# Two edits to a two-layer AdaLN program: the experts' back half moved into the next chunk's front, and a reciprocal root as one power on POOL

## What is computed

```python
h = _layernorm(x) * (1 + ca) + sa
x = x + ga * _L0_attn_ref(h, ...)
h = _layernorm(x) * (1 + cb) + sb
x = x + gb * _L0_ffn_ref(h, ...)

def _L0_attn_ref(x, ...):                 # 16 heads of 8
    x_norm = _layernorm(x, gamma, beta)
    q, k = x_norm @ w_q, x_norm @ w_k;  v = x @ w_v
    q = _l2_normalize(q);  k = _l2_normalize(k)          # per token and head: 64 norms a partition
    resonance = 0.5 + 0.5 * tanh((q k^T - 0.27) * 15)
    modulation = resonance * gate_q[..., :, None] * gate_k[..., None, :]
    return (modulation @ v) @ w_o + b_o

def _L0_ffn_ref(x, controller, f1, bias, f2):   # groups of 32 tokens, 32 experts x 4 sets = 128 slots
    logits = einsum('bgtd,des->bgtes', grouped, controller) + tie
    perm = (logits == max(logits, axis=-3))               # the token that each slot takes
    dispatched = einsum('bgtd,bgtes->bgesd', grouped, perm)
    inner = relu(einsum('bgesd,desf->bgesf', dispatched, f1) + bias)
    intermediate = einsum('bgesf,esfd->bgesd', inner, f2)
    return einsum('bgesd,bgtes->bgtd', intermediate, perm)
```

## Time and profile before

| | |
|---|---|
| median of 3 runs | 1460.92 us (1458.93 to 1463.24) |
| the profiled execution | 1462.04 us, its span 1460.0 us |
| mean granted clock | 0.916 |
| busy: PE, DVE, ACT, POOL | 85%, 75%, 65%, 36% of the span |
| first attention | about 24 to 446 us |
| experts | 446.6 to 724.3 us |
| second attention, second feed-forward part | behind it |

### The profile page before, as it was taken

One profiled execution on the slowest core, in us unless ns is written; L12 is line 12 of the kernel. 1 busy time (PEld: TensorE's weight loads), 2 busy tenths in 40 slices (PEclk: granted clock), 3 DMA queues, 4 the chain that ended last, 5 costly groups with the idle time before them and its releaser, 6 DMA issues. The chain is left out here.

```text
span 1460.0 us, 39907 instructions
## 1 busy us (share of the span) xinstructions
PE 1246.1 (85%) x13658; PEld 845.9 (58%) x13658; DVE 1090.6 (75%) x2971; ACT 949.6 (65%) x1308; POOL 526.1 (36%) x739
## 2 busy tenths in 40 slices
PE   2588888888885787787769999999937999999998
PEld 1345555555543667575635555555515877777776
DVE  2789999999965565655679999999746677777763
ACT  0388888888882534444428888888845666676675
POOL 1233333333321021211223333333304665565553
PEclk7699999999997797878769999999968999999999
DMA  3411111111001110100020000000000000000000
GB/s 81 149 35 34 32 32 32 32 32 32 25 9 47 29 36 11 45 3 16 2 91 17 12 14 14 14 11 14 12 3 1 8 15 7 14 14 14 7 15 23
DMA packets 44749, 37.82 MB, mean 26 GB/s; under 512 B 5008, under 2 KB 43472, under 8 KB 44144
## 3 DMA queue, kind: packets, MB, share of 16 engines
q1 hardware_dynamic: 44656, 36.56, 8.7%
HBM read 32.21 MB, written 4.34 MB: 25 GB/s over the span
## 5 line engine op out<-in xcount | busy, mean ns | idle before, releaser
L1960 ACT ACTIVATE a_probs<-psum_all 128x1024 f32<-128x1024 f32 x256 | 248.0, 1022 | 88.0 <-PE psum_all L1875 88.0
L474 ACT ACTIVATE probs<-psum_all,biases 128x1024 f32<-128x1024 f32 x256 | 270.9, 1113 | 45.8 <-PE psum_all L385 45.0
L2348 PE MATMUL psum_all<-ffn_hi,weights_r 128*128 128x512 f32 x704 | 286.5, 407 | 9.9 <-POOL ffn_lo L2308 5.7
L2348 PE MATMUL psum_all<-ffn_lo,weights_r 128*128 128x512 f32 x704 | 280.4, 398 | 0.0
L2308 POOL TENSOR_TENSOR ffn_lo<-ffn_full,ffn_hi 128x512 fp32r<-128x512 f32 x144 | 189.6, 1325 | 128.2 <-ACT ffn_hi L2433 87.6
L2348 PEld LDWEIGHTS psum_all<-ffn_hi,weights_r 128*128 128x128 f32 x704 | 133.6, 190 | 51.4 <-DVE ffn_full L2563 9.2
L2348 PEld LDWEIGHTS psum_all<-ffn_lo,weights_r 128*128 128x128 f32 x704 | 134.1, 190 | 28.6
L398 PE MATMUL psum_all<-probs,vpad 128*32 128x257 f32 x2048 | 140.4, 392 | 0.3 <-ACT probs L474 0.3
L1889 PE MATMUL psum_all<-a_probs,vpad 128*32 128x256 f32 x2048 | 137.0, 385 | 0.1
L2445 ACT ACTIVATE ffn_full<-psum_all,scales 128x512 f32<-128x512 f32 x128 | 88.2, 689 | 71.6 <-PE psum_all L2348 71.3
L2308 DVE TENSOR_TENSOR ffn_lo<-ffn_full,ffn_hi 128x512 fp32r<-128x512 f32 x64 | 55.0, 859 | 81.9 <-ACT ffn_hi L2448 81.9
(11 more groups left out here) (222 smaller groups left out, 2752.9 us busy)
## 6 DMA issues: line engine op xcount, KB each, us to landing
a_mod_gate<-modulation_table SPq DMA_DIRECT2D x64, 128.0 KB, 2.9
a_mod_norm<-modulation_table SPq DMA_DIRECT2D x32, 128.0 KB, 3.0
X<-in_x SPq DMA_DIRECT2D x32, 128.0 KB, 2.8
f<-in_f SPq DMA_DIRECT2D x2, 2048.0 KB, 10.1
e_mod_norm<-modulation_table SPq DMA_DIRECT2D x32, 128.0 KB, 2.9
out<-X SPq DMA_DIRECT2D x16, 256.0 KB, 2.3
e_gates<-modulation_table SPq DMA_DIRECT2D x32, 64.0 KB, 2.7
weights<-in_h SPq DMA_DIRECT2D x2, 1024.0 KB, 8.0
```

Source lines behind the costliest of these rows:

```text
L474: nc.scalar.activation(probs[:, c % 4, :, :, 0:T].rearrange("p r k q -> p (r k) q"), SC[c % 2].rearrange("p (a q) -> p a q", q=T), ACT.Tan ...
L1960: nc.scalar.activation(probs[:, c % 4, :, :, :].rearrange("p r k q -> p (r k q)"), SC[c % 2], ACT.Exp, scale=float(np.float32(1.0) / np.sq ...
L2348: ins = nc.tensor.matmul(dst, weights[:, w0:w0 + P], part[layer][:, k, :], start=first and i == 0, stop=last and i == len(parts) - 1)
```

## The change

In attention_0 the steps 2 to 9 of newton_step go. floor_norms keeps the first (with another scale), and a new POOL function root makes rnorm with one tensor_tensor of pow on 128x64. It stands in POOL's list between modulate(b+3) and gate_out(b). turned_out moves from the head of the next step to a place ahead of the splits. The two stacks become one tile whose parts are written by one cast, one subtraction and two copies. In experts_0 the chunks become one list of 42 steps without a loop: at step i the front works on batch i, and the back on chunk m with its work spread over 8 steps, s = (i - 9) mod 8. first_matrices lie in s 0 and 1, second_matrices in s 2 and 3, turn_back and hand_back in s 4 to 7. The turns of h and of the choice share a bank and one copy; scores and outputs share a bank; takenT, sent and given are kept twice, h and mod_norm four times instead of eight. The slots are numbered set first, so that results_out writes 8 neighbouring columns.

```diff
+            def root(n):
+                pool.wait_ge(norm2c_done, n + 1)
+                wait(pool, qkn_done, n)
+                wait(pool, gate_in_done, n)
+                nc.gpsimd.tensor_tensor(rnorm[:, :], norm2c[:, :], minus_half[:, :], ALU.pow).then_inc(rnorm_done, 1)
...
                     norm_1(b + 3)
                     modulate(b + 3, 1 - p)
+                if there(b + 2):
+                    root(b + 2)
                 if there(b):
                     gate_out(b, p)
...
+            def floor_norms(n):
+                dve.wait_ge(norm2_done, n + 1)
+                wait(dve, rnorm_done, n)
+                nc.vector.tensor_scalar(norm2c[:, :], norm2[:, :], NORM_FLOOR, SPLIT_SCALE ** -2, ALU.max, ALU.mult).then_inc(norm2c_done, 1)
 
             def scale(n):
-                dve.wait_ge(newton, n * RSQRT_STEPS + RSQRT_STEPS)
+                dve.wait_ge(rnorm_done, n + 1)
...
-                nc.vector.tensor_copy(qstack[p][:, :, 0:4:2, :], twice(0))
-                nc.vector.tensor_copy(kstack[p][:, :, 0:2, :], twice(1)).then_inc(hi_done, 1)
+                nc.vector.tensor_copy(part(p, 0), normed()).then_inc(hi_done, 1)
...
-                nc.vector.tensor_tensor(qstack[p][:, :, 1:4:2, :], twice(0), qstack[p][:, :, 0:4:2, :], ALU.subtract)
-                nc.vector.tensor_tensor(kstack[p][:, :, 2:4, :], twice(1), kstack[p][:, :, 0:2, :], ALU.subtract).then_inc(stacks_done, 1)
+                nc.vector.tensor_tensor(part(p, 1), normed(), part(p, 0), ALU.subtract).then_inc(lo_done, 1)
+
+            def double(n, p):
+                dve.wait_ge(lo_done, n + 1)
+                nc.vector.tensor_copy(stack[p][:, 1, :, 2:4, :], stack[p][:, 1, :, 0:2, :])
+                nc.vector.tensor_copy(stack[p][:, 0, :, 3:1:-1, :], stack[p][:, 0, :, 0:2, :]).then_inc(stacks_done, 1)
...
-                newton_of(1)
+                if next_:
+                    floor_norms(b + 2)
                 if new:
                     keys_out(b + 1, 1 - p)
-                newton_of(2)
...
                 if next_:
                     scale(b + 2)
                     gate_sums(b + 2)
+                if ahead:
+                    turned_out(b + 3, 1 - p)
+                if next_:
                     split_high(b + 2, p)
                     split_low(b + 2, p)
+                    double(b + 2, p)
```

TensorE's list of the experts after the change, and the new results_out and SP order:

```diff
+            for i in range(STEPS):
+                m, s = back(i)
+                before, at = back(i - 1)
+                if i <= B:
+                    turn(i)
+                if at in QUARTERS:
+                    hand_back(before, 2 * (at - 4) + 1, min(i, B))
+                if s in (0, 1):
+                    first_matrices(m, 2 * s)
+                    first_matrices(m, 2 * s + 1)
+                if s in (2, 3):
+                    second_matrices(m, 2 * (s - 2), min(i - 1, B))
+                if s in QUARTERS:
+                    turn_back(m, 4 * (s - 4))
+                    turn_back(m, 4 * (s - 4) + 1)
+                if front(i):
+                    score(i)
+                if front(i - 1):
+                    send(i)
+                if s in (2, 3):
+                    second_matrices(m, 2 * (s - 2) + 1, min(i, B))
+                if s in QUARTERS:
+                    turn_back(m, 4 * (s - 4) + 2)
+                    turn_back(m, 4 * (s - 4) + 3)
+                    hand_back(m, 2 * (s - 4), min(i + 1, B))
...
-                last = copy(given[:, :, slots].rearrange("p g e -> p e g"), given_banks(r)[s].rearrange("p (e g) -> p e g", g=CG))
+                last = copy(given[m % 2][:, :, slot:slot + EB], B_SLOTS[s].rearrange("p (e g) -> p g e", g=CG))
...
+            for n in range(HB):
+                load(n)
+            load_gates(0)
+            for n in range(HB, B):
+                if n % CB_ == 0 and n >= 3 * CB_:
+                    load_gates(n // CB_ - 2)
+                load(n)
```

More of the change, by code:

```diff
@@ L872, in _, with load, load_gates @@
-            for j in range(HB):
-                load(0, j)
-            chunk(0)
-            with sp.Fori(1, NCHUNK - 1) as c:
-                chunk(c)
-            chunk(NCHUNK - 1)
+            def load(n):
+                wait(sp, mod_loaded, 16 * n)
+                wait(sp, h_done, n - HB + 1)
+                sp.dma_start(mod_norm[n % HB][:, :, :], rows_of(n, ROW_CB0, 2)).then_inc(mod_loaded, 16)
+            def load_gates(m):
+                wait(sp, delta_done, m * CB_)
+                for j in range(CB_):
+                    sp.dma_start(gates[:, j, :], rows_of(m * CB_ + j, ROW_GB0, 1)).then_inc(gates_loaded, 16)
@@ L993, in _ @@
-            chunk(0)
-            with pe.Fori(1, NCHUNK - 1) as c:
-                chunk(c)
-            chunk(NCHUNK - 1)
-        def results_out(eng, copy, done, c, r, s0):
-            wait(eng, given_psum, c * ROUNDS + (r + 1))
+            for i in range(STEPS):
[13 more added lines that the diff above has]
+                    turn_back(m, 4 * (s - 4) + 1)
+                if front(i):
+                    score(i)
+                if front(i - 1):
+                    send(i)
[5 more added lines that the diff above has]
+                    hand_back(m, 2 * (s - 4), min(i + 1, B))
@@ L1055, in _, with front_out, sent_out @@
-            chunk(0)
-            with act.Fori(1, NCHUNK - 1) as c:
-                chunk(c)
-            chunk(NCHUNK - 1)
+            def front_out(i):
+                wait(act, turned, i + 1)
+                wait(act, logits_psum, i - 1)
+                wait(act, sent_psum, i - 2)
+                part = slice(0 if front(i) else T, 2 * T if front(i - 1) else T)
+                nc.scalar.copy(hT_taken[i % 2][:, part], bank[0][:, part]).then_inc(turned_done, 1)
+            def sent_out(n):
+                wait(act, sent_psum, n + 1)
+                wait(act, turned_back, (n // CB_ - 1) * TB_)
+                by_group = psum[:, 4 * 512:8 * 512].rearrange("p (g n) -> p n g", g=TG)
+                for t in range(TT):
+                    g0 = (n % CB_ * TT + t) * TG
+                    last = nc.scalar.copy(sent[n // CB_ % 2][:, :, g0:g0 + TG], by_group[:, t * SLOTS:(t + 1) * SLOTS, :])
+                last.then_inc(sent_done, 1)
@@ L1060, in _, with root @@
         @block.gpsimd
         def _(pool):
-            def root(c, j):
-                n = count(c, j)
+            def root(n):
                 wait(pool, moments_done, n + 1)
@@ new lines, in _ @@
+            wait(dve, w_loaded, 16 * len(dram["experts_loads"]))
+            centre(0)
+            for n in range(2):
+                modulate(n)
+                centre(n + 1)
+            for i in range(STEPS):
+                m, s = back(i)
+                before, at = back(i - 1)
+                if at in QUARTERS:
+                    gate(before, 2 * (at - 4) + 1)
+                if s in (0, 1):
+                    add_bias(m, 2 * s)
+                    add_bias(m, 2 * s + 1)
+                if s in (2, 3):
+                    results_out(dve, nc.vector.tensor_copy, given_dve, m, 2 * (s - 2), 0)
+                if s in QUARTERS:
+                    turned_out(dve, nc.vector.tensor_copy, givenT_dve, m, 4 * (s - 4))
+                if front(i + 2):
+                    modulate(i + 2)
+                if front(i):
+                    choose(i)
+                if s in QUARTERS:
+                    turned_out(dve, nc.vector.tensor_copy, givenT_dve, m, 4 * (s - 4) + 2)
+                    gate(m, 2 * (s - 4))
+                if front(i + 3):
+                    centre(i + 3)
+                if s in (2, 3):
+                    results_out(dve, nc.vector.tensor_copy, given_dve, m, 2 * (s - 2) + 1, 0)
```

486 lines of the change are left out of this document (197 added, 289 removed).

## The result

The kernel after takes 1758.07 us (median of 4 runs, 1754.84 to 1763.53), the one before 1459.93 us beside it (4 runs, 1458.87 to 1463.24): ratio 1.204, interval 1.200 to 1.208. The prediction was 1733 us, slower, with case A's own range of 1650 to 1830 and a range for 8 in 10 of 1440 to 1840.

A forecast was written before the change was run, and what follows sets the result against it. No engine was taken as full; a loop between TensorE and VectorE bounds the attention. Profiled 1462.0 us + 322 (attention) - 50 (experts) = 1734, so median 1733; 8 in 10 range 1440 to 1840.

The forecast's parts named there:

- case A: Attention, the forecast itself: the power costs by the column, 10.1 us for 64; 1733 us in all, chance 0.68.
- Part 1, the power: Attention, POOL: one 64-column power replaces eight VectorE steps and takes 10.1 us, from a line through widths 2 and 4.
- the addition's pace: POOL: columns beyond the first cost 2.1 ns each, as in a plain addition, so the 64-column power takes 0.83 us.
- B: Rival, attention: the power is cheaper by the column in a long run, about 5 us; step 16 us, 1537 in all; chance 0.12.
- C: Rival, attention: the power costs 0.83 us; step 11.0 us, 1374 us in all; chance 0.17.
- Part 2, the loop: Attention: work queued behind root on POOL waits, so the step becomes 22.2 us against 12.15; +322 us over 32 roots.
- Part 3, the splits: Attention, VectorE: one cast, one subtraction and two copies take 1.7 us instead of 2.0, covered by TensorE's projection.
- Part 4, the experts: Experts: the back of one chunk overlaps the front of the next; 227 us against 277.7, -50 us.
- 24 shared steps at 6.3 us: Experts: steps with front and back together, TensorE 5.9 us plus 0.4 for waits; 151 us in all.
- The first front, 40.2 us: Experts: the first chunk's front alone, from 446.6 to L925 at 486.78 us in the profile of before.
- The last back, 36 us: Experts: the last chunk's back alone, 38.7 us less 4 for the results and plus 1 for fewer banks.
- Rival D: Experts: the overlap does nothing or harms, the stage stays at 278 us; 1783 us with the 10.1 us power; no separate chance.

The follow-up runs named there:

- widths2: Kernel before with ten more POOL instructions in its setup, powers on 2 to 128 columns and multiplications on 2, 64 and 128: 1486.91 us.
- root_mult: Kernel after with root as a multiplication of the same operands instead of a power, not a usable result: 1403.14 us, ratio 0.959.
- root_32: Kernel after with the power on 32 of root's 64 columns and a multiplication on the rest, not a usable result: 1596.2 us.
- newton_after: Kernel after without the power, the nine newton steps back on VectorE, the last two between and behind the halves of xn: 1418.88 us, ratio 0.970.
- layout_only: Kernel before with only the slots numbered set first, so results_out writes runs of 8 columns, no overlap: 1446.82 us, ratio 0.992.

## Why the prediction was right, and where it was off

**Part 1, the power.** Right. 10.56 us against 10.1, between the ends. The choice of the line through the two widths over the addition's pace decided the case. The slope was 160 ns a column and not 153: from 2 to 4 columns is a short base to draw a line from. The rule of the Trainium skill (GPSIMD Engine Reference, section Performance versus the Vector engine: about 2.6 cycles an element for a tensor_tensor of two inputs) fits the multiplications of widths2 (2.1 ns a column) and not the powers (160 ns). Rivals B and C, which needed a power of 5 us and of 0.83 us, are out with the 10.56 us of L523. root_mult, C's case made by force, did give C's step, 10.95 against 11.0; its 1403 us against C's 1374 is the experts' missing gain. B's loop held too: with the 5.7 us of root_32 its sum gives 5.7 + 10.1 + 1 = 16.8, and that step is 16.98.

**Part 2, the loop.** Right in its order and nearly in its size. Counted from the start of a root, the forecast and two neighbouring steps (the second has its values at 342.63 and the next root at 345.41 in VectorE's and POOL's timelines):

| | forecast | step at 301.05 | step at 322.64 |
|---|---|---|---|
| power ends | 10.1 | 10.6 | 10.6 |
| xn ends | 12.9 | 13.3 | 13.3 |
| values start | 19.4 | 18.8 | 20.0 |
| next root | 22.2 | 21.6 | 22.8 |

Up to xn the chain ran 0.4 us late because of the power. For TensorE coming back cold I had taken "slow at first and fast at the end"; the real loop does the faster and the slower kind by turns, and their means are 19.4 for the values and 22.2 for the step, the forecast. That the means agree to a tenth is luck: neither kind is the step that I summed, and the 0.4 us that the chain is late at xn is made up behind it, where the sum had 6.5 us and the two steps take 5.5 and 6.7. With the clock up throughout the sum said 20.3; no step in the middle of the loop is that short. TensorE's idle before the turn was put at 9 us and is 9.7; VectorE's waits were put at some 8 us and are 322.3 / 31 = 10.4. The attention's sum is +309 against +322: the step of before had been counted as 12.15 from one pair of rows (which in fact start 12.19 apart), where its mean is 12.26, and the mean of after is 22.06 with the shorter steps at the loop's ends. That makes 0.25 x 32 = 8; most of the rest is one interval fewer (31, -9.8), less the 5 us that filling and draining add.

**Part 3, the splits.** 0.45 + 0.73 and two copies at about 0.20 each, 1.6 us against 1.7, and covered. What I said of hT and xnT, that moving them would fill idle time of the old loop, fits newton_after, which is 0.85 us a step shorter than the kernel before; the move is one of three things that differ there.

**Part 4, the experts.** Mis-sized: -15 in place of -50. The step that held is results_out: 0.69 us a copy forecast, 0.685 measured on VectorE, and layout_only shows that this term brings 13.9 of the 15 us. These failed:
- 24 shared steps at 6.3 us. They took 173.5 / 24 = 7.2. TensorE's busy time was put at 5.9 and is 152.87 / 24 = 6.4, since the clock came to 0.83 and not to the 0.88 which 5.9 supposes; the waits were put at 0.4, and TensorE's idle is 0.86. Together +22 us. All of it lies in the six steps with second matrices, with their waits for the four banks: from turn to turn they took 66.3 us, 11.0 each, and the other 18 took 6.0 each, less than forecast.
- The first front, 40.2 us, taken over unchanged from before. It took 43.5 (756.0 to 799.5): the turns of the choice and of h now go through one chain with the copy, and from the fourth batch on each takes 3.6 to 3.8 us from turn to turn, where the kernel before took 2.3 to 3.3. In each such step TensorE stands 0.68 us for the copy and 0.48 us for the choice. The shared bank and copy, which the forecast counted as a saving, thus seem to cost time here; that was read from the waits and not tried.
- The last back, 36 us. It took 46.5. I gave +1 us for the fewer banks; with one set of four, every round behind the first stands 1.6 to 1.7 us for the copies of the round before, and its matmuls run cold, 18.9 us for the four rounds against 7.5 in layout_only:

```profile
987.32 3.69 PE L936 MATMUL psum_all<-e_relued,f 32*128 32x64 f32 x64 [1.59 <-DVE e_slots L998]
...
992.71 3.69 PE L936 MATMUL psum_all<-e_relued,f 32*128 32x64 f32 x64 [1.70 <-DVE e_slots L998]
```

Rival D, that the experts' overlap does nothing, was thus nearly right for its mechanism. It put the stage at 278 because it left out the copies' own gain.

**The sum.** 1734 for the profiled execution, 1756.4 measured: -13 from the attention, +35 from the experts. The two errors have opposite signs; the total fits better than its parts.

## What to carry to other kernels

Before an operation moves to an engine that seems idle, look for its price by the element in rows of the same operation, and not of the same instruction type: two widths of it give a slope, and here that slope decided 300 us. What an instruction holds up is what is queued behind it, and if its result closes a loop, moving it in the queue only changes the name of the wait. An overlap brings only what buffers of its own allow: where both halves share a set of banks, each step takes the waits of both, and here TensorE's clock was low behind the gaps.

## What the chip showed that I had not expected

- A copy of 512 fp32 columns out of PSUM took 1239 ns on VectorE and 1286 ns on ScalarE when it wrote single scattered columns, and 685 and 587 ns when it wrote runs of 8 (before and layout_only). The order of the slots in memory, a matter of the host's layout, was worth 14 us.
- The granted clock fell to 0.50 in the experts in a stretch of which TensorE was busy 82% (821 to 831 us), with gaps of about 0.5 to 1.2 us between its matmuls. Twelve transposes without use per step held it at full in three chunks (1.00 from 474.70 to 491.60), and did not bring it back in the last, where it stayed at 0.50 from 626.7 to 647.2 us with TensorE busy 96%.
- A power on POOL costs 158 to 160 ns a column from 8 to 128 columns, 75 times the 2.1 ns of a multiplication, and does not get cheaper in a long run.
- The same attention took 22.06 us a step in one execution and 22.28 in another: how often TensorE's clock is back by the time of the projection differs between executions (17 and 20 slow ones in 32 steps).
